# Four-layer graph kernel, attention sweep of the first layer: the row maxima in one list of slots over the units, their mask bias in a unit of its own, the gate weights in eight single loads

## The reference, cut to what matters

```
hW  = h @ W                                   # per head
e   = leaky_relu(concat(hp, hm) @ a)          # a score for each node
att = where(edge_adj != 0, e[None, :], NEG)   # row i sees the scores of its neighbours
att = softmax(att, axis=1)
out_head = (att * edge_adj) @ hW
```

## Time and profile before

| | |
|---|---|
| time, median of 3 (lowest to highest) | 2252.53 us (2251.53 to 2253.24) |
| span of the profiled execution, first to last instruction | 2246.4 us |
| device time of that same execution | not reported on its own; its span is 6.1 us under the median |
| PE busy in the span | 94% |
| DVE, ACT busy in the span | 69%, 42% |
| the attention sweep of the first layer | 418.6 to 1066.2 us |

### The profile page before, as it was taken

One profiled execution on the slowest core, in us unless ns is written; L12 is line 12 of the kernel. 1 busy time (PEld: TensorE's weight loads), 2 busy tenths in 40 slices (PEclk: granted clock), 3 DMA queues, 4 the chain that ended last, 5 costly groups with the idle time before them and its releaser, 6 DMA issues.

```text
span 2246.4 us, 26319 instructions
## 1 busy us (share of the span) xinstructions
PE 2101.5 (94%) x9738; PEld 1157.4 (52%) x9747; DVE 1555.7 (69%) x2623; ACT 949.8 (42%) x1459; POOL 118.3 (5%) x169
## 2 busy tenths in 40 slices
PE   7999999799999988889999999999899987999996
PEld 4556665344444454445555534556899962222232
DVE  4665547696967577743678863444899957879987
ACT  2222215687878687855222210001021246544342
POOL 0000000000000000000001010000010030002011
PEclk9999999899999999999999999999899988999997
DMA  7665634455454545553000034451110115323231
GB/s 235 217 206 181 217 102 195 155 178 183 170 191 142 183 156 199 171 181 127 1 0 1 0 90 129 131 130 27 51 33 20 38 40 194 87 85 90 71 86 39
DMA packets 133167, 265.56 MB, mean 118 GB/s; under 512 B 15258, under 2 KB 62904, under 8 KB 130200
## 3 DMA queue, kind: packets, MB, share of 16 engines
q1 hardware_dynamic: 114712, 234.50, 33.1%
q10 hardware_dynamic: 18324, 29.34, 3.5%
HBM read 220.43 MB, written 43.36 MB: 117 GB/s over the span
## 4 chain that ended last, share of the span: by engine, by line
PE 61%; DVE 22%; ACT 11%; issue 4%; DMA 2%; SPq 1%; POOL 0%; DVEq 0%; ACTq 0%; POOLq 0%
PE banks L1034 13%; PE banks L937 9%; PE banks L1085 9%; PE banks L1150 8%; PE banks L1119 6%; PE banks L1161 4%; ACT arena L1266 4%; DVE arena L1658 3%; PE banks L926 3%; DVE arena L2013 3%; ACT arena L1302 2%; DVE arena L2085 2%; PE banks L978 2%; PE banks L849 2%; ACT arena L1295 1%
## 5 line engine op out<-in xcount | busy, mean ns | idle before, releaser
L1034 PE MATMUL banks<-arena 128*128 128x512 f32 (+2 forms) x1512 | 598.1, 553 | 45.1 <-DVE arena L1741 45.1
L1034 PEld LDWEIGHTS banks<-arena 128*128 128x128 f32 x1512 | 286.0, 193 | 346.4 <-issue 266.3
L1741 DVE TENSOR_TENSOR arena<-arena 128x1536 f32<-128x1536 f32 (+4 forms) x132 | 201.5, 1527 | 173.6 <-ACT arena L1302 147.0
L2085 DVE SCALAR_TENSOR_TENSOR arena<-arena 128x1024 f32<-128x1024 f32 (+3 forms) x264 | 293.6, 1180 | 33.1 <-PE banks L1161 25.9
L1150 PE MATMUL banks<-arena 128*64 128x512 f32 (+3 forms) x1056 | 222.5, 561 | 13.0 <-DVE arena L2085 12.9
L1119 PE MATMUL banks<-arena 128*124 128x129 f32 (+2 forms) x1936 | 219.1, 275 | 10.6 <-DVE arena L2013 10.5
L937 PE MATMUL banks<-arena 128*128 128x512 f32 (+4 forms) x528 | 225.7, 549 | 0.2 <-ACT arena L1207 0.2
L1119 PEld LDWEIGHTS banks<-arena 128*124 128x124 f32 (+2 forms) x1936 | 216.1, 187 | 13.6 <-issue 7.5
L1085 PE MATMUL banks<-arena 128*128 128x512 f32 (+4 forms) x528 | 207.4, 547 | 5.0 <-DVE arena L1842 3.7
L1658 DVE CUSTOM_DVE_ANT_0 arena<-arena 128x2708 f32<-128x2708 bf16 (+1 forms) x66 | 196.3, 2974 | 3.3 <-DVE arena L1652 3.3
L1295 ACT ACTIVATE arena<-arena 128x512 f32<-128x512 f32 (+4 forms) x264 | 162.2, 660 | 80.1 <-PE banks L1034 77.5
(11 more groups left out here) (223 smaller groups left out, 2214.3 us busy)
## 6 DMA issues: line engine op xcount, KB each, us to landing
arena<-hw_rows SPq DMA_DIRECT2D x126, 384.0 KB, 3.2
arena<-adj_T SPq DMA_DIRECT2D x126, 256.0 KB, 3.3
arena<-in_adj SPq DMA_DIRECT2D x17, 1354.0 KB
arena<-in_adj SPq DMA_DIRECT2D x42, 512.0 KB
adj_T<-arena ACTq DMA_DIRECT2D x63, 256.0 KB, 2.2
arena<-adj_T SPq DMA_DIRECT2D x84, 192.0 KB, 3.1
arena<-in_adj SPq DMA_DIRECT2D x15, 1024.0 KB
arena<-in_adj SPq DMA_DIRECT2D x15, 768.0 KB
```

The lines of the kernel that those rows point to most:

```text
L1034: ins = PE.matmul(bank(2 * (c % 2) + f)[:, 0:wid(c)], hs[0:R, m % 3, h * D + f * P:h * D + (f + 1) * P], E[0:R, n % 3, h, 0:wid(c)], start ...
L1741: V.tensor_tensor(e, e, a, ALU.mult).then_inc(s["p_ok"], 1)
L2085: V.scalar_tensor_tensor(PM3[0:k, n % 3, h, 0:w], r3_bc[0:k, h, c * WW:c * WW + w], smalls[0:k, 4, h * T + t:h * T + t + 1], mask3[0:k, n ...
```

## The change

`side_slot` goes, and with it the rule by chunk. A table `ROWS_AT` gives for each row tile four units: the bias in the first, the three heads in the other three (row tile 4 has bias and head 0 both in unit 1). The list runs from unit 1 to unit 88, across the chunk edges. By chunk it puts 15, 14, 14, 10, 1 and 0 heads and 5, 5, 5, 3, 0 and 0 biases; before it was 12, 12, 9, 9, 12 and 0 heads and 4, 4, 3, 3, 4 and 0 biases. The load of row tile i + 1 is issued one unit after the last head of row tile i. `denominators` stand at t = 16 and `shifts` at t = 17 of every chunk but the last. The eight loads of the gate weights are issued one each behind units 92, 94, ... 106; the wait for all exponentials stands ahead of the first.

```diff
-def side_slot(c, t):
-
-    if c + 1 < CH and t // 4 < tiles_in(c + 1):
-        return FIRST_TILE[c + 1] + t // 4, t % 4
-    return None, 3
+ROWS_AT = {4: (1, 1, 2, 3), 5: (4, 5, 6, 7), 6: (8, 9, 10, 11), 7: (12, 13, 14, 15), 8: (17, 18, 20, 21),
+           9: (22, 23, 24, 26), 10: (27, 28, 29, 30), 11: (31, 32, 33, 34), 12: (36, 37, 38, 40), 13: (41, 42, 43, 44),
+           14: (46, 47, 48, 49), 15: (50, 51, 52, 54), 16: (55, 56, 57, 58), 17: (59, 60, 61, 62), 18: (64, 65, 66, 67),
+           19: (69, 70, 72, 74), 20: (76, 77, 79, 81), 21: (83, 84, 86, 88)}
+BIAS_AT = {at[0]: i for i, at in ROWS_AT.items()}
+HEAD_AT = {at[1 + h]: (i, h) for i, at in ROWS_AT.items() for h in range(H0)}
+LOAD_AT = {ROWS_AT[i][H0] + 1: i + 1 for i in range(RPC, T - 1)}
+SHIFTS_AT = 16
+ROWS_END = ROWS_AT[T - 1][H0]
+PIECES_AT = range(ROWS_END + 4, (CH - 1) * T, 2)
...
+        def gate_piece(sp, k):
+            if k == 0:
+                sp.wait_ge(b_exp, H0 * T)
+            i = k // 2
+            if k % 2 == 0:
+                load(sp, g_wn[:, i], (e_Wih, e_Whh, n_Wih, n_Whh)[i].rearrange("(g p) k -> p g k", p=P), g_in)
+            else:
+                load(sp, g_bias[:, i], (e_bih, e_bhh, n_bih, n_bhh)[i].partition_broadcast(P), g_in)
...
                 unit_loads(sp, n)
-                if c + 1 < CH:
-                    i, h = side_slot(c, t)
-                    if h == 0 and t:
-                        row_load(sp, i)
-                    if t == 17 and c + 2 < CH:
-                        row_load(sp, FIRST_TILE[c + 2])
-                    if t == 20:
-                        maxima_row(sp, c + 1)
-                if c == CH - 2 and t == 18:
-                    sp.wait_ge(b_exp, H0 * T)
-                    ... (the eight loads)
+                if n in LOAD_AT:
+                    row_load(sp, LOAD_AT[n])
+                if c + 1 < CH and t == 20:
+                    maxima_row(sp, c + 1)
+                if n in PIECES_AT[0:8]:
+                    gate_piece(sp, PIECES_AT.index(n))
... (ACT)
-                    if t and side_slot(c, t - 1)[1] < H0:
-                        weights(*side_slot(c, t - 1), general)
-                    if c + 1 < CH and t == 4 * tiles_in(c + 1):
+                    if n - 1 in HEAD_AT:
+                        weights(*HEAD_AT[n - 1], general)
+                    if c + 1 < CH and t == SHIFTS_AT:
                         denominators(c + 1)
... (DVE; row_bias is the bias taken out of row_head as it was)
-                    i, h = side_slot(c, t)
-                    if h < H0:
-                        row_head(i, h, general)
-                    if c + 1 < CH and t == 4 * tiles_in(c + 1):
+                    if n in BIAS_AT:
+                        row_bias(BIAS_AT[n], general)
+                    if n in HEAD_AT:
+                        row_head(*HEAD_AT[n], general)
+                    if c + 1 < CH and t == SHIFTS_AT + 1:
                         shifts(c + 1)
```

More of the change, by code:

```diff
@@ L162, in __init__ @@
         self.landed = sum(16 if j // (LOADS * 2) < CH - 1 else 32 for j in range(self.buf, i + 1, WIDE))
-def side_slot(c, t):
-    if c + 1 < CH and t // 4 < tiles_in(c + 1):
-        return FIRST_TILE[c + 1] + t // 4, t % 4
-    return None, 3
+ROWS_AT = {4: (1, 1, 2, 3), 5: (4, 5, 6, 7), 6: (8, 9, 10, 11), 7: (12, 13, 14, 15), 8: (17, 18, 20, 21),
[3 rows of a table added]
+assert sorted(ROWS_AT) == list(range(RPC, T))
+BIAS_AT = {at[0]: i for i, at in ROWS_AT.items()}
+HEAD_AT = {at[1 + h]: (i, h) for i, at in ROWS_AT.items() for h in range(H0)}
+LOAD_AT = {ROWS_AT[i][H0] + 1: i + 1 for i in range(RPC, T - 1)}
+SHIFTS_AT = 16
+assert all(ROWS_AT[i][H0] < (chunk_of(i) - 1) * T + SHIFTS_AT for i in ROWS_AT)
+ROWS_END = ROWS_AT[T - 1][H0]
+PIECES_AT = range(ROWS_END + 4, (CH - 1) * T, 2)
 def build(nc, x, adj, gat_W, gat_a, e_Wih, e_Whh, e_bih, e_bhh, n_Wih, n_Whh, n_bih, n_bhh,
@@ L684, in _ @@
                 unit_loads(sp, n)
-                if c + 1 < CH:
-                    i, h = side_slot(c, t)
-                    if h == 0 and t:
-                        row_load(sp, i)
-                    if t == 17 and c + 2 < CH:
-                        row_load(sp, FIRST_TILE[c + 2])
-                    if t == 20:
-                        maxima_row(sp, c + 1)
-                if c == CH - 2 and t == 18:
-                    sp.wait_ge(b_exp, H0 * T)
-                    for i, (w, b) in enumerate(((e_Wih, e_bih), (e_Whh, e_bhh), (n_Wih, n_bih), (n_Whh, n_bhh))):
-                        load(sp, g_wn[:, i], w.rearrange("(g p) k -> p g k", p=P), g_in)
-                        load(sp, g_bias[:, i], b.partition_broadcast(P), g_in)
+                if n in LOAD_AT:
[4 more added lines that the diff above has]
+                    gate_piece(sp, PIECES_AT.index(n))
             sp.wait_ge(g_wok, 16)
@@ L1646, in _, with row_bias @@
             glink = Chain(dve, gen_link)
+            def row_bias(i, general):
+                dve.wait_ge(b_diag, i - RPC + 1)
+                link(V.tensor_scalar(mbias[0:kp(i), :], arow[0:kp(i), :], 0.0, NEG, ALU.is_equal, ALU.mult))
+                if not general:
+                    dve.sem_inc(b_rowfree, 1)
             def row_head(i, h, general):
@@ L1649, in row_head @@
                 bias = mbias_first[:, i] if i < RPC else mbias
[L1650 to L1654, removed]
                 if j >= 2:
```

## The result

| | before | after |
|---|---|---|
| median, lowest to highest | 2252.0 (2251.0 to 2253.2), 4 runs | 2214.8 (2210.5 to 2216.3), 4 runs |
| ratio of the runs | 1 | 0.983, 95% interval 0.9815 to 0.9843 |
| span of the profiled execution | 2246.4 | 2213.4 (its own time 2215.1) |
| PE idle before its products (L1034; after L1044) | 45.1 us | 19.8 us |

The account below looks back on a forecast made before the run. PE is busy nearly throughout, so only its waits or slower clock can be won: 7.0 + 2.6 + 3.1 - 0.8 + 26.1 = 38.0 us off the 2246.4 span gives 2208.4, plus 6.1 is 2214.5 us; range 2205 to 2225, 8 in 10.

Parts of the forecast that it names:

- chunk 0, start and edge: First chunk of the sweep: PE's gap before unit 1 goes, 0.7 us edge added; 113.9 for 120.9 us.
- chunk 1: Second 512-column chunk: floor 110.2 us plus up to 1.5 at unit 44; 111.7 for 114.3 us.
- chunk 2: Third 512-column chunk: at PE's floor, no edge gap at unit 66; 110.2 for 113.3 us.
- chunk 3: First 384-column chunk: ten heads, almost every second unit, plus logarithm; 97.1 for 96.3 us, no gain.
- chunk 4: Second 384-column chunk: one head left, gate loads spread; 84.4 for 110.5 us, including 0.9 for clock.
- Start: Units 0 to 2: without a bias in unit 0, PE's 4.00 us gap and the slower clock behind it go.
- The logarithm: At t = 16, behind a head's exponential in chunks 0, 1 and 3: 2.82 us on ACT with two table loads.
- The gap at unit 44: Edge behind a short tail unit: clips and head's exponential line up, store low after the logarithm; up to 1.5 us.
- The gate loads: Chunk 4: one load every second unit should flow beside the work, removing 6.73 us of gap and 2.6 in clock.
- Row loads: Some biases wait up to a us for POOL without cost to PE; a load 3.6 us longer would begin to count.
- PE's idle time: Before its products, near 15 us in place of 45, nearly all between units 67 and 89, longest at 83 and 88.
- What lies around the span: Outside the profiled span: the median of the runs was taken to stand 6.1 us over it.

Follow-up runs that it names:

- second profile: The changed kernel run once more, unaltered, beside later experiments on one chip: 2213.3 us, ratio 0.9827 to the kernel before.

## Why the prediction was right, step by step

| step | predicted | measured |
|---|---|---|
| chunk 0, start and edge | 113.9, saves 7.0 | 113.2, saves 7.7 |
| chunk 1 | 111.7, saves 2.6 | 112.5, saves 1.8 |
| chunk 2 | 110.2, saves 3.1 | 111.9, saves 1.3 |
| chunk 3 | 97.1, costs 0.8 | 97.4, costs 1.1 |
| chunk 4 | 84.4, saves 26.1 | 83.9, saves 26.6 |
| sum | 38.0 | 36.3 |

*Start.* As forecast: unit 1 follows at once, and unit 2's multiplication at 430.4 is in time for PE at 433.9. Chunk 0 came out 0.7 us under the forecast here and 0.5 us over it in the second profile, mostly by how long PE ran slowly at its start.

*Chunk 3.* The reader can check the two durations that the sum rests on, in DVE's timeline of the changed kernel, multiplications of units 72 to 74:

```profile
784.45 1.36 DVE L1752 TENSOR_TENSOR arena<-arena 128x1152 f32<-128x1152 f32 x1 [2.22 <-ACT arena L1312]
789.15 1.36 DVE L1752 TENSOR_TENSOR arena<-arena 128x1152 f32<-128x1152 f32 x1
793.06 1.36 DVE L1752 TENSOR_TENSOR arena<-arena 128x1152 f32<-128x1152 f32 x1 [2.22 <-ACT arena L1312]
```

4.70 us with the head, 3.91 behind it, as in the earlier trace rows. Alternating, a pair costs 8.61 us against PE's 7.74. That is why ten heads spread over 22 units cost as much as the nine packed into twelve did. The logarithm, on ACT:

```profile
827.09 2.56 ACT L1276 ACTIVATE arena<-arena 128x2708 f32<-128x2708 f32 x1 [0.85 <-DVE arena L1680]
829.75 1.28 ACT L1282 ACT_TABLE_LOAD   x1
831.27 1.28 ACT L1312 ACT_TABLE_LOAD   x1
832.57 1.17 ACT L1312 ACTIVATE arena<-arena 128x1152 f32<-128x1152 f32 x1
```

From the first load to the exponential 2.82 us, as before. The 2.66 us that the Trainium skill gives for one switch (ScalarE: Activation LUTs, What ACT_TABLE_LOAD costs) would by estimate need 5.3 for the two here; the measurement decides.

*Chunk 2 is the step that was mis-sized.* The gap at unit 44 came (predicted up to 1.5 us, measured 1.75), but the clock behind it was left out, and it took another 1.7 us of chunk 2 (94.79 us for the 18 units that took 93.11 in the kernel with row tile 4 earlier). The prediction had allowed for it at unit 88 only, where in the first profile it did not come: unit 88 took 4.11 us behind 2.32 us of gap, and in the second profile 1.5 us more behind 2.7.

*The gate loads* flowed as forecast. Two strips of chunk 4 were late (DVE waited 3.0 us at unit 97 and 3.2 us at the tail unit 109) and DVE's lead covered both.

*Row loads.* DVE waited for POOL once, by 0.3 us, at row tile 15 (in the second profile by 2.1 us, at row tile 4), and PE did not stall for it.

*PE's idle time* was put near 15 us and measured 19.8. Both this number and the 45.1 before hold the 6.6 us ahead of unit 0, which the forecast's parts leave out; without them it is 13.3 us, of which 11.1 lie between units 67 and 89, the longest at 83 and 88 as forecast.

*What lies around the span* was wrong. The profiled run after has 1.7 us around its span, not the 6.1 that the prediction took from a median and another run's span. The profiled execution before was also an uncommonly short one: its span of 2246.4 is under all 18 spans of that kernel on record from the later sets (2247.7 to 2255.3). The span predicted (2208.4) was 5 us short of the 2213.4 measured, and the median 0.3 us off; that agreement is luck, two errors of 4 to 5 us against each other. Of the 5 us, 1.7 are the chunks' sum, 2.8 a later start of the sweep (see the last section), and 0.5 lie behind it.

## What to carry to other kernels

Work that runs beside a paced engine is best priced by the time from one hand-over to the next with and without it, for each unit width, and then placed: a side step can be free in the unit where its engine would wait for another anyway, and lengthens the chain beside a second one: here the 17 biases of 1.75 us cost 16.5 us when they stood beside a head. Put such work where the paced engine's unit is long, not evenly; where its unit is shorter than the side step, leave free units ahead of it. Large loads that nobody awaits soon delayed the small ones behind them here, and computing ahead did not cover that: split them, and count how many us of room each load has, since one place later may be past it.

## What the runs showed of the hardware

**The clock of TensorE is not the same from run to run in the same place.** All these kernels have the same instructions up to the sweep, yet the first product of the sweep began at 418.6 us before, and at 421.4, 420.8, 419.3, 418.0, 422.1, 417.2, 422.0 and 420.6 in the profiles after. PE's last six products ahead of the sweep, in the kernel before, the changed kernel's first and second profile, and the kernel with the logarithm moved:

```profile
409.27 2.82 PE L1018 MATMUL banks<-arena 128*128 128x512 f32 x6 [2.89 <-DVE arena L1684]
409.40 5.46 PE L1028 MATMUL banks<-arena 128*128 128x512 f32 x6 [2.90 <-DVE arena L1695]
407.84 2.82 PE L1028 MATMUL banks<-arena 128*128 128x512 f32 x6 [2.90 <-DVE arena L1695]
411.26 4.28 PE L1028 MATMUL banks<-arena 128*128 128x512 f32 x6 [2.90 <-DVE arena L1695]
```

The busy time from 409.2 to 415 us of the first two, with the columns of the earlier trace rows:

```profile
409.20:415.00 5.80, 2.82 (x6) 1.05 (x6) 2.90 (x5) 2.82 (x7) 0.00 (x0) 0.95 0.45 136
409.20:415.00 5.80, 5.46 (x6) 1.85 (x6) 1.36 (x4) 1.39 (x4) 0.00 (x0) 0.50 0.41 132
```

The same six products behind the same gap took 2.82, 4.28 or 5.46 us, and where they took 5.46 the granted clock was 0.50, that is 1.2 GHz. That is 2.6 of the 2.8 us by which the sweep of the changed kernel began later. The rest of the spread (407.8 to 411.4 us at the start of these six) lies further ahead, and its cause stays open: from 330 to 345 us the granted clock was 0.77 in the profile that began its sweep at 417.2 and in the one that began at 422.1.

In the sweep, gaps of 1.75 and 2.35 us were followed by a unit 1.7 to 1.8 us longer, and gaps of 1.75 us (unit 44 with row tile 4 earlier) and 2.32 us (unit 88) were not. The 2.75 us at unit 83 were followed by a unit of 5.78 us in the changed kernel and by one of 4.11 us with the bias beside head 0. So the length of a gap alone does not tell, among gaps of 1.75 to 2.8 us; behind each such gap some 1.7 us may be lost or not. That fits the 1 to 11 us between the lowest and highest time of one kernel, while the chunk lengths of the changed kernel's two profiles agree to 1.2 us; how much of that spread it makes was not measured.
